# Splitting the operands of the expert up products of layer 2, and spreading the late recurrence over the blocks

## The reference, cut to what matters

```
combine_w = top-2 of softmax(x @ gate_weight.T), normalised       # [1024, 8]
for each expert:
    gate, up = split(x @ gate_up_proj.T)        # 256 -> 512 and 512
    y = (silu(gate) * up) @ down_proj.T         # 512 -> 256
    out += combine_w[:, e] * y
```

## Time and profile before

| | |
|---|---|
| time, median of 3 runs | 474.77 us (474.06 to 475.88) |
| the profiled execution: its time | 475.86 us |
| its span in the trace | 473.9 us |
| busy share of the span: PE, DVE, ACT, POOL | 86%, 72%, 49%, 51% |
| layer 2's blocks, first gate_up to the end of the last block_down | 265.5 to 413.1 us |

### The profile page before, as it was taken

The page is one execution under the profiler, slowest core; times in us unless marked ns, Lnnn a source line. Parts: engine busy times, 40 slices in busy tenths (PEclk is TensorE's granted clock), DMA queues, the critical chain, the costliest instruction groups (busy, mean ns, idle before and its releaser), DMA issues. The chain is left out here.

```text
span 473.9 us, 5880 instructions
## 1 busy us (share of the span) xinstructions
PE 405.2 (86%) x1685; PEld 255.1 (54%) x1685; DVE 342.2 (72%) x620; ACT 232.9 (49%) x460; POOL 243.6 (51%) x341
## 2 busy tenths in 40 slices
PE   2576899999999999957784789999999999985995
PEld 1465678655455555625552345655566555652563
DVE  5999887999999999789958347547645411028895
ACT  4600376267677667648874123232233233329784
POOL 6444032478688997333002646775775464215442
PEclk9999999999999999979996899999999999999899
DMA  7900001555465752000020898889889986050001
GB/s 234 391 1 0 1 2 47 222 179 174 166 221 184 214 197 96 1 1 1 2 90 21 284 417 301 300 313 343 312 317 356 297 294 251 24 189 0 12 33 44
DMA packets 23262, 77.37 MB, mean 163 GB/s; under 512 B 3424, under 2 KB 7904, under 8 KB 19648
## 3 DMA queue, kind: packets, MB, share of 16 engines
q1 hardware_dynamic: 19936, 69.94, 41.6%
q0 software_dynamic: 2208, 6.03, 4.1%
q10 hardware_dynamic: 1088, 1.05, 0.7%
HBM read 71.76 MB, written 5.24 MB: 162 GB/s over the span
## 5 line engine op out<-in xcount | busy, mean ns | idle before, releaser
L1879 PE MATMUL bank<-gu,xbT 128*128 128x512 f32 x184 | 83.3, 595 | 4.0 <-issue 2.1
L1673 PE MATMUL bank<-hx,w2raw 128*128 128x512 f32 x128 | 67.2, 606 | 4.2 <-DVE hx L1228 3.3
L1428 DVE TENSOR_TENSOR hm<-bank,sl 128x512 f32<-128x512 f32 x23 | 15.9, 691 | 70.5 <-PE bank L1879 36.8
L763 ACT ACTIVATE rl<-bank 128x512 f32<-128x512 f32 x64 | 38.1, 595 | 40.1 <-PE bank L1537 39.0
L1879 PEld LDWEIGHTS bank<-gu,xbT 128*128 128x128 f32 x184 | 34.4, 190 | 39.0 <-issue 35.9
L1535 PE MATMUL bank<-xlhi,w1hi 128*128 128x512 f32 x64 | 49.3, 771 | 0.0
L1899 PE MATMUL bank<-dn,hT 128*128 128x256 f32 x184 | 45.2, 388 | 3.4 <-ACT hT L884 0.7
L454 POOL TENSOR_TENSOR fw<-fw,bw 128x256 f32<-128x256 f32 x32 | 24.5, 766 | 42.6 <-DVE bw L1032 42.2
L1228 DVE TENSOR_TENSOR hx<-bank,cwb 128x512 f32<-128x512 f32 x64 | 42.0, 658 | 4.8 <-ACT bank L767 4.7
L536 POOL DMA_INDIRECT y_rows<-yb,dest_i x23 | 25.5, 1110 | 35.7 <-ACT yb L890 34.6
L1037 DVE RECIPROCAL fw<-fw 128x256 f32<-128x256 f32 x24 | 41.5, 1730 | 0.0
(11 more groups left out here) (296 smaller groups left out, 911.4 us busy)
## 6 DMA issues: line engine op xcount, KB each, us to landing
gu<-in_gu SPq DMA_DIRECT2D x23, 1024.0 KB
cwb<-cw_rows SPq DMA_DIRECT2D x32, 512.0 KB, 3.8
dn<-in_dn SPq DMA_DIRECT2D x23, 512.0 KB, 4.7
traw<-in_t SPq DMA_DIRECT2D x3, 1024.0 KB
w1raw<-in_w SPq DMA_DIRECT2D x8, 256.0 KB, 4.9
w2raw<-in_w SPq DMA_DIRECT2D x8, 256.0 KB, 4.8
kT<-in_kt SPq DMA_DIRECT2D x4, 256.0 KB, 4.7
x<-in_x SPq DMA_DIRECT2D x2, 512.0 KB, 6.8
```

The source lines that it names most:

```text
L763: act.activation(rl[:, u % 3, :], bank[u % 4][:], ACT.Relu).then_inc(sem("r_ready"), 1)
L1673: pe.matmul(bank[4 + s][:], w2raw[:, e // 4 % 2, e % 4, :], hx[:, 0, u % 4, :], start=(e == 0), stop=(e == E0 - 1), skip_group_check=True) ...
L1879: ins = pe.matmul(bank[2 * (b % 2) + up][:], xbT[:, b % 2, k, :], gu[:, b % RING, k, up * I2:up * I2 + I2], start=(k == 0), stop=(k == KC ...
```

## The change

The up products of layer 2 are computed as three float32r terms, as layer 0 does it.

- **Weights.** ACT copies gu of block b to a float32r buffer `guhi` (`weights_high`, two instructions of 1024 columns; two buffers, one each for even and odd blocks). DVE subtracts it from gu in place for the first 1024 and the next 512 columns (`weights_low`, into `gulo`, which lies over gu), POOL for the last 512 (`weights_low_rest`).
- **Rows.** ACT's copy `xbT` becomes float32r, and DVE subtracts it from the bank (`rows_low`, 256 columns, into `xbTlo`).
- **PE.** gate_up is 12 float32r matmuls of 512 columns where it was 4 float32 ones; it waits for `xbT_low`, `gu_low` and `gu_rest`, no longer for the DMA itself.
- **Order.** ACT does weights_high(b+2) in step b between block_turned(b+1) and block_y(b-1). DVE does block_h(b), rows_low(b+1), weights_low(b+2) and then one task of the late recurrence. POOL does weights_low_rest(b+2) after scatter_block(b-2).
- **Late recurrence.** Its tasks (two scans of a denominator, two scans of a numerator, or reciprocal and product) are laid out in a list `LATE`, one for each step 1 to 21, one before the loop's end and two before the loop.
- **Ternary sums** move from DVE, steps 2, 8, 14, to ACT (an Abs with an accumulated sum over 2048 columns), steps 3, 9, 15, behind weights_high. Softmax and top-2 weights move ahead of the loop on DVE. SP's order is as before. Semaphores of layers 1 and 3 are merged, and buffers laid out anew.

```diff
+LATE[0] += [(0, 0), (0, 1)]
+for n, task in enumerate(((1, 0), (0, 2), (1, 1), (2, 0), (1, 2), (2, 1), (3, 0), (2, 2), (3, 1), (4, 0), (3, 2), (4, 1),
+                          (5, 0), (4, 2), (5, 1), (6, 0), (5, 2), (6, 1), (7, 0), (6, 2), (7, 1))):
+    LATE[n + 1] += [task]
+LATE[23] += [(7, 2)]
...
+            def weights_low_rest(b):
+                pool.wait_ge(sem("gu_high"), 2 * b + 2)
+                pool.tensor_tensor(gulo[:, b % RING, 1, SPLIT:2 * I2], gu[:, b % RING, 1, SPLIT:2 * I2], guhi(b)[:, 1, SPLIT:2 * I2].bitcast(F32), ALU.subtract
+                                   ).then_inc(sem("gu_rest"), 1)
...
             for b in range(RING):
                 gather_block(b)
+            weights_low_rest(0)
+            weights_low_rest(1)
...
                 if b >= 2:
                     scatter_block(b - 2)
-                if b < 2 * NBLK:
-                    late_sum(b // 2, 1 - b % 2, ("den", "num")[b % 2])
-                    if b % 2 and b // 2 + 1 < NBLK:
-                        late_value(b // 2 + 1)
+                if b + 2 < NB:
+                    weights_low_rest(b + 2)
+                for i, part in LATE[b]:
+                    if part < 2:
+                        late_sum(i, 1 - part, ("den", "num")[part])
+                        if part == 1 and i + 1 < NBLK:
+                            late_value(i + 1)
...
+            def weights_high(b):
+                act.wait_ge(sem(f"gu_in{b % RING}"), 16 * (b // RING + 1))
+                wait(act, sem("up_done"), b - 1)
+                for k in range(KC):
+                    act.activation(guhi(b)[:, k, :], gu[:, b % RING, k, :], ACT.Copy).then_inc(sem("gu_high"), 1)
+
+            def ternary_sum(m):
+                act.wait_ge(sem("t_in"), 16 * m + 16)
+                act.activation(tw[:, m, :], traw[:], ACT.Abs, accum_out=ws[:, 9 + m:10 + m]).then_inc(sem("tsum_part"), 1)
+
+            weights_high(0)
             block_turned(0)
...
                 if b + 1 < NB:
                     block_turned(b + 1)
+                if b == 0:
+                    weights_high(1)
+                if b + 2 < NB:
+                    weights_high(b + 2)
+                if b in (3, 9, 15):
+                    ternary_sum((3, 9, 15).index(b))
                 if b >= 1:
                     block_y(b - 1)
...
+            def rows_low(b):
+                dve.wait_ge(sem("xbT_ready"), b + 1)
+                dve.tensor_tensor(xbTlo[:, b % 2, :, :], xb_bank(b).rearrange("p (k c) -> p k c", k=KC),
+                                  xbT[:, b % 2, :, :].bitcast(F32), ALU.subtract).then_inc(sem("xbT_low"), 1)
+
+            def weights_low(b):
+                for k, n in ((0, 2 * I2), (1, SPLIT)):
+                    dve.wait_ge(sem("gu_high"), 2 * b + k + 1)
+                    dve.tensor_tensor(gulo[:, b % RING, k, 0:n], gu[:, b % RING, k, 0:n], guhi(b)[:, k, 0:n].bitcast(F32), ALU.subtract).then_inc(sem("gu_low"), 1)
...
+            for task in LATE[0]:
+                late_task(*task)
+            weights_low(0)
+            rows_low(0)
+            softmax()
+            top2_weights()
             for b in range(NB):
                 if b in (4, 10, 16):
                     ternary_round((4, 10, 16).index(b))
-                if b < 2 * NBLK:
-                    late_scan(b // 2, 2 * (b % 2))
-                    late_scan(b // 2, 2 * (b % 2) + 1)
                 block_h(b)
...
+                if b + 1 < NB:
+                    rows_low(b + 1)
                 if b == 0:
-                    softmax()
-                if b == 1:
-                    top2_weights()
-                if b in (2, 8, 14):
-                    ternary_sum((2, 8, 14).index(b))
+                    weights_low(1)
+                if b + 2 < NB:
+                    weights_low(b + 2)
+                for task in LATE[b + 1]:
+                    late_task(*task)
...
             def turn_block(b):
                 pe.wait_ge(sem(f"xb_in{b % RING}"), 16 * (b // RING + 1))
-                wait(pe, sem("xbT_ready"), b)
+                wait(pe, sem("xbT_low"), b)
...
-                pe.wait_ge(sem("xbT_ready"), b + 1)
-                pe.wait_ge(sem(f"gu_in{b % RING}"), 16 * (b // RING + 1))
+                pe.wait_ge(sem("xbT_low"), b + 1)
+                pe.wait_ge(sem("gu_low"), 2 * b + 2)
+                pe.wait_ge(sem("gu_rest"), b + 1)
...
-                    for k in range(KC):
-                        ins = pe.matmul(bank[2 * (b % 2) + up][:], xbT[:, b % 2, k, :], gu[:, b % RING, k, up * I2:up * I2 + I2],
-                                        start=(k == 0), stop=(k == KC - 1))
+                    cols = slice(up * I2, up * I2 + I2)
+                    terms = [(rows[:, b % 2, k, :], w[:, k, cols]) for rows, w in
+                             ((xbT, guhi(b)), (xbT, gulo[:, b % RING, :, :]), (xbTlo, guhi(b))) for k in range(KC)]
+                    for n, (rows, w) in enumerate(terms):
+                        ins = pe.matmul(bank[2 * (b % 2) + up][:], rows, w, start=(n == 0), stop=(n == len(terms) - 1))
```

More of the change, by code:

```diff
@@ L50 @@
 ROUTED = {"mk": 2, "lsub": 3, "slab": 4, "rows": 5, "dest": 6, "weights": 8}
+SPLIT = 512
+LATE = [[] for _ in range(24)]
+LATE[0] += [(0, 0), (0, 1)]
[3 more added lines that the diff above has]
+LATE[23] += [(7, 2)]
+TILES = {"": 0, "3": NT}
 SUMMED = {"place": 1, "rows": 2, "dest": 3}
@@ L103, in build @@
         cursor[0] = turned
-        diag = sb("diag", [P, 2 * NT, P])
+        guhi0 = sb("guhi0", [P, KC, 2 * I2], F32R)
         assert cursor[0] <= turned + KC * TOK * 4
@@ L165, in build @@
         cursor[0] = region
+        gulo = sb("gulo", [P, RING, KC, 2 * I2], F32R)
+        cursor[0] = region
         gu = sb("gu", [P, RING, KC, 2 * I2])
@@ L180, in build @@
         hT2 = sb("hT2", [P, 2, I2 // P, P])
+        masks = cursor[0]
         lane_of = sb("lane_of", [P, 2 * NT, P], F16)
@@ L183, in build @@
         r2c = sb("r2c", [P, 2, NT, E2 * E2])
-        xbT = sb("xbT", [P, 2, KC, P])
+        masks_end = cursor[0]
+        cursor[0] = masks
+        diag = sb("diag", [P, 2 * NT, P])
+        assert cursor[0] <= masks_end
+        cursor[0] = masks_end
+        xbT = sb("xbT", [P, 2, KC, P], F32R)
         slot_end = cursor[0]
@@ L210, in build @@
         cw2p = sb("cw2p", [P, 2, NT])
+        xbTlo = sb("xbTlo", [P, 2, KC, P], F32R)
+        guhi1 = sb("guhi1", [P, KC, 2 * I2], F32R)
+        assert cursor[0] <= ends[0]
         ends.append(cursor[0])
@@ L239, in gain_bank, with guhi @@
             return bank[((0, 1, 1, 7), (0, 1, 6, 2), (0, 1, 2, 3), (0, 2, 1, 3))[l][b]]
+        def guhi(b):
+            return (guhi0, guhi1)[b % 2]
         def x3_bank(b):
@@ L500, in _, with quant_rows @@
                                        ).then_inc(sem("q_quant"), 1)
-            def quant_rows(t, scale, known, ready, free, rows=TH):
+            def quant_rows(t, scale, known, ready, free, rows=TH, done=0):
                 p = t % 2
                 pool.wait_ge(sem(known), t // rows + 1)
-                wait(pool, sem(free), t - 1)
+                wait(pool, sem(free), done + t - 1)
                 pool.tensor_scalar(qf[:, p, :], cond[:, t, :], scale[:, t:t + 1], ROUND, ALU.mult, ALU.add
@@ L626, in quant3 @@
             def quant3(t):
-                quant_rows(t, st[:, 8, :], "c3_scale", "q13_ready", "q1t3_ready", 2)
+                quant_rows(t, st[:, 8, :], "c3_scale", "q13_ready", "q1t_ready", 2, NT)
             half = st[:, 11, 0:2]
@@ L814, in l1_second @@
                 p = t % 2
-                wait(act, sem("m2_ready" + tag), t - 1)
+                wait(act, sem("m2_ready"), TILES[tag] + t - 1)
                 for h in range(2):
-                    act.wait_ge(sem("q2t_ready" + tag), 2 * t + h + 1)
+                    act.wait_ge(sem("q2t_ready"), 2 * (TILES[tag] + t) + h + 1)
                     act.activation(q2T[:, p, 4 * h:4 * h + 4, :], bank[5 + h][:], ACT.Copy, bias=-ROUND
-                                   ).then_inc(sem("q2T_ready" + tag), 1)
+                                   ).then_inc(sem("q2T_ready"), 1)
             l1_first(0)
@@ L917, in l3_first @@
                 p = t % 2
-                act.wait_ge(sem("q1t3_ready"), t + 1)
+                act.wait_ge(sem("q1t_ready"), NT + t + 1)
                 wait(act, sem("m13_ready"), 2 * t - 2)
-                act.activation(qT[:, p, :, :], bank[4][:, 0:C], ACT.Copy, bias=-ROUND).then_inc(sem("q1T3_ready"), 1)
+                act.activation(qT[:, p, :, :], bank[4][:, 0:C], ACT.Copy, bias=-ROUND).then_inc(sem("q1T_ready"), 1)
             def l3_silu(t):
@@ L1439, in late_scan, with late_task @@
                                            0.0, ALU.add, ALU.mult).then_inc(sem("scan_num" if part == 3 else "scan_den"), 1)
+            def rows_low(b):
[6 more added lines that the diff above has]
```

(26 more changed lines are left out.)

10 lines of the change are left out of this document (2 added, 8 removed).

## The result

| | before | changed |
|---|---|---|
| median of the runs | 475.32 us (474.06 to 479.94) | 543.38 us (542.58 to 544.87) |
| span of the profiled execution | 473.9 us | 542.7 us |
| S(4), start of gate_up(4) | 291.6 | 304.6 |
| S(22) | 403.9 | 471.7 |

The changed kernel takes 1.1418 times as long, 95% interval 1.1372 to 1.1465: 68 us more, where the prediction has 33. S(b) is the start of gate_up(b), as in the prediction. Nearly the whole difference lies in layer 2's blocks: S(22) is 67.8 us later, and 2.3 of these are there at S(0). The direction is as forecast; the time is above the range of 487 to 526 us.

The account below looks back on a forecast made before the run. PE bounds the kernel before; after the change a two-block loop through gu's DMA, ACT and DVE does, 14.3 us. Start, nine loops and two ternary extras put S(22) 33.6 us later; less 0.6, 508 us, range 487 to 526.

Parts of the forecast that it names:

- PE's part: Layer 2's gate_up on PE: 12 matmuls at 0.235 us, 2.82 us, 0.6 less; a block 5.57 us if PE bounds.
- ACT's copy held by gu: In layer 2, ACT reaches weights_high(b+2) at about S(b) + 4 and stands until gu lands at S(b) + 7.9.
- The start: Layer 2's first blocks: split weights and late landing of gu(2) put S(0) at about 267, S(2) at 284.
- plain pairs: Two blocks of layer 2 without a ternary step: a loop from gu through ACT and DVE, 14.3 us with collisions.
- the ternary sums: ACT's sum behind weights_high delays gate_up(4), (10), (16): a 12.2 us step, 3.5 us extra for second and third.
- DVE's loop: Layer 2's two-block loop through weights_low, a late task, block_h and rows_low on DVE: 13.65 us before collisions.
- Flight time: Layer 2's DMA of gu from issue to landing: between 5.5 and 7.3 us, 6.5 taken.
- ACT's way: Layer 2's two-block loop through ACT: weights_high, block_y, silu and hT copies behind gu's landing, 13.2 us.
- Collisions of DVE and POOL: Layer 2's two-SBUF-input operations on DVE and POOL delay each other: 0 to 1.28 us per loop, 0.65 taken.
- rival C's addition: PE's idle stretches in layer 2 drop its clock to the 1.2 GHz level; most of this hidden in idle time.
- C: Heavy rival: DVE pays 1.28 us every loop plus late_sum on POOL, layer 2 loops of 16 us, 521 us; chance 0.18.
- A: Rival: gu lands early, ACT never stands, PE sets layer 2's pace at 5.57 us per block, 469 us; chance 0.06.

Follow-up runs that it names:

- e12: Changed kernel without splitting the weights from block 3 on, so layer 2's outputs leave out the real weights: 476.74 us, ratio 1.0002.
- e1: Changed kernel with gu of block b+1 ahead of dn of block b in the SP queue: 506.61 us, ratio 1.0631.
- e8: Kernel before the change with only the late recurrence's tasks spread over all blocks: 476.86 us, ratio 1.0018.
- e9: Changed kernel with the second and third ternary weight tensors (traw) fetched two SP steps later: 528.34 us, ratio 1.1121.
- e6: e5 with DVE subtracting all columns of gulo and POOL none: 483.90 us, ratio 1.0152.
- e3: Changed kernel with DVE subtracting all 2048 columns of gulo, POOL none: 534.17 us, ratio 1.1147.
- e5: e1 with ternary total, rounding, clipping and write one block later, second and third fetch two later, rounding right behind rows_low: 504.46 us, ratio 1.0599.
- e11: e10 with gu(2) ahead of dn(0) and dn(1), and block 1's high and low parts earlier on ACT and DVE: 480.89 us, ratio 1.0110.
- e10: e6 with rows_low of block b+1 ahead of block_h(b) on DVE: 482.69 us, ratio 1.0129.
- e2: Changed kernel with ACT's ternary sum ahead of weights_high of the same step: 545.24 us, ratio 1.1463.

## Why the prediction was wrong, point by point

**Right.** PE's part: blocks of 5.54 us where PE is the bound (e12; predicted 5.57), gate_up 2.8 us at full clock. PE is busy 70% of the stretch from 304 to 475 us (predicted under 80%). ACT's copy held by gu, with silu and the hT copies behind it: 65.5 us of waits, and e1. gu(b+2) issued 1.3 us after S(b) (318.98 against 317.67, predicted 1.4). The spread recurrence is free in the kernel before (e8). The start: S(2) at 285.0 for 284.

**Where the 34 us are.** From S(4) to S(22) the forecast had seven plain pairs of blocks at 14.3 us and two with a ternary step at 17.8.

| part | predicted | measured | difference |
|---|---|---|---|
| S(4) | 301.8 | 304.6 | +2.8 |
| seven plain pairs | 100.1 | 109.3 (13.1 to 19.6) | +9.2 |
| pairs 8 to 10 and 14 to 16 | 35.6 | 28.2 + 29.6 = 57.8 | +22.2 |

The sum is 34.2, which is S(22) at 471.7 for 437.5.

**The step that failed: "the ternary sums", 3.5 us beyond a plain pair for each of two, where 14.6 were measured.** It followed ACT and PE and never looked at SP, where `traw` and gu stand in one queue. The second tensor's fetch waits for POOL's write of the first, POOL runs late in the changed kernel, and so gu(9) is issued at S(7) + 8.1 where the sum has 1.4; gu(15) likewise. This wait doesn't stand in the earlier trace rows, and it is no stall of a compute engine, so nothing in the trace of before pointed to it but the order of the calls. It is 16.2 us in the trace; taking it out of the changed kernel gives 15 (e9), which is the larger part of the 22.2. The prediction also has these pairs as 5.6 + 12.2; the 5.6 became 14.5 and 16.3, the 12.2 became 13.6 and 13.3.

**Rounding and clipping on DVE.** The seven plain pairs aren't alike: 13.1, 19.6, 13.3, 18.4, 13.4, 16.1 and 15.4 us. The second, fourth and sixth have the clipping of a ternary tensor in them and are 11.2 us above the forecast together; the other four are 2.0 us below it. Three of these four follow a ternary step, during which the next gu lands, so that ACT doesn't stand for it. The prediction gives rounding (1.3 us) and clipping (1.2 us) no time in DVE's loop. They did no harm before, when DVE was busy 45 of 99 us. Now the clipping stands ahead of block_h(6) and rows_low(7), and the next low part meets POOL:

```profile
326.65 1.20 DVE L1470 TENSOR_SCALAR traw<-traw 128x2048 f32<-128x2048 f32 x1
...
328.69 4.25 DVE L1497 TENSOR_TENSOR gulo<-gu,guhi 128x1024 fp32r<-128x1024 f32 x2
```

The same two rows come back 60 us later (1.20 and 4.25, at 386.57 and 388.62). What the clipping costs by itself was not tested.

**Flight time.** 6.5 was taken, the median is 7.6; gu(8) took 7.1 (326.1 - 319.0), gu(7) 8.1 and gu(9) 7.8. The median also lies beyond my upper bound of 7.3. ACT's way starts at the landing, so about 1 us goes into every loop that nothing else holds up. How the 9.2 us of the plain pairs are shared between flight, clipping and collisions was not measured.

**Collisions of DVE and POOL.** Bounds 0 and 1.28 us, 0.65 taken. The subtractions at line 1497 and the scans by their shapes, in the stretch of the blocks:

```profile
L1497 DVE TENSOR_TENSOR gulo<-gu,guhi 128x512 fp32r<-128x512 f32 x23 | 36.8, 1598 | 0.0
...
L1497 DVE TENSOR_TENSOR gulo<-gu,guhi 128x1024 fp32r<-128x1024 f32 x22 | 32.5, 1479 | 52.3 <-ACT guhi L931 52.3
...
L1486 DVE TENSOR_TENSOR_SCAN bw<-ekk,dec 128x255 f32<-128x255 f32 x14 | 15.1, 1076 | 0.0
L1484 DVE TENSOR_TENSOR_SCAN fw<-dec,ekk 128x256 f32<-128x256 f32 x14 | 13.3, 951 | 0.0
```

Undisturbed they take 0.68, 1.18 (half of the pair of 2.35 in e6), 0.66 and 0.68 us. So a pair of low parts costs 1.60 + 1.48 - 1.86 = 1.2 us extra, nearly the upper bound, and a pair of scans 0.7 more, which the sum left out. e3 and e6 take out the part that POOL's subtraction causes: 10 us with gu late, 20 us with gu early, where this is the bound. One place shows the form of it:

```profile
264.52 2.89 DVE L1497 TENSOR_TENSOR gulo<-gu,guhi 128x1024 fp32r<-128x1024 f32 x2 [1.03 <-ACT guhi L931]
265.52 1.35 POOL L565 TENSOR_TENSOR gulo<-gu,guhi 128x512 fp32r<-128x512 f32 x1 [1.13 <-ACT guhi L931]
```

DVE's first part takes 1.2 us and the second is recorded from 265.7 on for 1.75, where 0.68 is usual: 1.07 us too long. It lies beside POOL's operation (to 265.52 + 1.35 = 266.87) for 1.2 us. Nearly the whole overlap is lost, which looks like waiting to the end and not like sharing. The Trainium skill (SBUF — State Buffer, section "SBUF: two separate sides") says just this, that the pair of ports is locked for a whole instruction and not shared; the prediction weighed it against rows of partial overlap and chose the middle. These rows agree with the page on that. They don't bear out "whichever starts first", as the prediction has it: at 328.69 DVE's part of 1024 columns is recorded 0.05 us ahead of POOL's and takes 3.11 us for 1.18, while POOL's operations beside it keep their usual 1.29 and 0.73. Operations with an input in PSUM (rows_low, 0.41 us; block_h, 0.68) keep their time beside POOL too (0.66 at 283.96, 0.41 at 290.65), as its condition of two SBUF inputs has it.

**The clock, rival C's addition.** Said to be mostly hidden; it isn't. Behind 6.8 us of idle, block_down(7) took 3.75 us where 1.97 is usual and it lies between the hT copies and gate_up(9). After S(0), S(1), S(4), S(7), S(10), S(14), S(16) and S(22) gate_up takes 4.5 to 5.1 us from its first start to its last end, where 3.06 is usual (0.43 us from matmul to matmul for 0.235; the granted clock is 0.50 from 328.9 to 331.4 us, the 1.2 GHz level). What share of the 34 us this is was not measured by itself: no run changes the clock and nothing else.

**The rivals.** The mechanism of C (long loops, with nearly full collisions and a low clock) is nearest, but its 521 us lacks SP's wait and the clipping as well. A fell, though e12 shows its arithmetic: with no copy to wait for, PE does set 5.5 us per block. Even then the slower start eats the gain.

**What stays open.** The terms don't add: SP's wait is worth 15 us with gu late (e9) and about 2 with gu early (e5 against e1, which shifts the ternary work too), and DVE's work may be what stands behind it there. In e6 every third block takes 7.4 to 7.6 us, each time one with a reciprocal and product on DVE; in e11 these still take 6.5 to 7.8, and I have no run that says whether DVE's sum of work or the order of the tasks does it.

## What to carry to other kernels

When an engine gets an instruction that waits for a DMA, everything behind it in its order inherits the flight time, so first ask who issues that DMA, what stands ahead of it in that queue, and who releases that: here two swapped lines on SP were worth 37 us. Work shared out to an idle POOL isn't free when DVE's operation reads SBUF twice and POOL's reads SBUF too: count the whole POOL instruction as time that DVE may lose, and try DVE alone. Work that an engine did for nothing while it had slack (here rounding and clipping) has to be priced anew when the change takes the slack. And price a faster matmul form by the preparation of its operands: here 0.6 us per block on PE stood against 2.1 us of ACT and 1.9 to 2.4 us of DVE.

## What the runs showed that was not expected

A two-input operation on DVE can wait for POOL far longer than it lasts: the scan of 2.92 us in e5 does 0.68 us of work beside three POOL operations in a row, and that of 2.30 us at 334.01 lies beside POOL's 2.27 us ternary write, which has one SBUF input. DVE's reciprocal, with one input, kept its 1.74 us beside a POOL operation (348.56 in the changed kernel). A 1 MB fetch took 7.6 us (median of 23) in a kernel whose three stretches above had the DMA engines busy only 31 to 71% of the time, no less than the 7.3 us worked out for a busy stretch. By the other runs it is what stands ahead of it, more than the mean load, that makes the difference: in those that issue gu ahead of dn and have a median for it, it is 5.9 us (e6) and 5.6 (e10, e11), though the DMA engines are busier there (74% in e6), and in those with dn 1.1 us ahead it is 7.1 (e2) to 7.8 (e12). The row of e11:

```profile
gu<-in_gu SPq DMA_DIRECT2D x23, 1024.0 KB, 5.6
```

So e1's edit may have gained by a shorter flight as well as by an earlier issue; its own trace has no median for gu.
